# A new preamble for a fused attention and expert kernel: order of loads, rows shared with ScalarE, constant scales, gate bias in bfloat16 parts

## What is computed

```python
def _L0_conv_ref(pair_rep, ln_w, ln_b, wq, wk, wv, wb, wg_w, wg_b, wrep_w, wrep_b):
    x = (pair_rep - mu) * jax.lax.rsqrt(var + EPS) * ln_w + ln_b      # mu, var over all of it
    q, k, v = proj(wq), proj(wk), proj(wv)                            # B, NH=4, C=32, 128, 128
    g = jax.nn.sigmoid(proj(wg_w) + wg_b.reshape(1, NH, C, 1, 1))
    bias = jnp.einsum('hc,bcij->bhij', wb, x)
    scores = jnp.einsum('bhcij,bhcik->bhijk', q, k) * scale + bias[:, :, None, :, :]
    o = g * jnp.einsum('bhijk,bhcik->bhcij', jax.nn.softmax(scores, axis=-1), v)
    return jnp.einsum('oc,bcij->boij', wrep_w, o) + wrep_b.reshape(1, C_Z, 1, 1)

x = x + _L0_conv_ref(_ln_c(x), ...)       # _ln_c: each row of 128, eps 1e-6
t = _to_tokens(x)
t = t + _L0_ffn_ref(_ln_t(t), ...)        # top 2 of 8 experts, 128 -> 512 -> 128, gelu
```

## Time and profile before

| | us |
|---|---|
| median of three runs | 913.08 (911.72 to 914.72) |
| the profiled execution, its own time | 913.78 |
| its span in the trace | 912.0 |
| busy in it: TensorE, VectorE, ScalarE, GpSimd | 621.5, 693.4, 583.5, 416.9 |

### The profile page before, as it was taken

The page is one execution under the profiler, slowest core; times in us unless marked ns, Lnnn a source line. Parts: engine busy times, 40 slices in busy tenths (PEclk is TensorE's granted clock), DMA queues, the critical chain, the costliest instruction groups (busy, mean ns, idle before and its releaser), DMA issues. The chain is left out here.

```text
span 912.0 us, 21482 instructions
## 1 busy us (share of the span) xinstructions
PE 621.5 (68%) x6804; PEld 509.6 (56%) x6804; DVE 693.4 (76%) x2423; ACT 583.5 (64%) x1517; POOL 416.9 (46%) x556
## 2 busy tenths in 40 slices
PE   0006699999998889888888510048999999999100
PEld 0001388877777677776776410047888888888100
DVE  3699579999988998998898369038888888888153
ACT  0015489998998899788878451047788778778100
POOL 3000112221156423545645548717777777777400
PEclk9999689997999899889988555579999999999755
DMA  9933691000000000000000002122322322322499
GB/s 198 222 81 68 193 91 3 3 2 1 2 23 28 26 1 11 26 26 25 31 23 31 28 30 84 45 60 67 84 81 77 83 77 83 81 80 68 92 203 282
DMA packets 61683, 62.01 MB, mean 68 GB/s; under 512 B 20708, under 2 KB 51493, under 8 KB 59912
## 3 DMA queue, kind: packets, MB, share of 16 engines
q1 hardware_dynamic: 51592, 34.28, 18.4%
q0 software_dynamic: 8704, 17.98, 5.9%
q10 hardware_dynamic: 1280, 8.39, 4.2%
HBM read 36.18 MB, written 25.26 MB: 67 GB/s over the span
## 5 line engine op out<-in xcount | busy, mean ns | idle before, releaser
L773 ACT ACTIVATE L<-L,lmin 128x128 f32<-128x128 f32 x512 | 159.6, 398 | 0.2
L700 POOL DMA_INDIRECT expert_out<-yo,rows_all x142 | 140.4, 989 | 41.6 <-issue 21.9
L652 POOL DMA_INDIRECT routed<-pay,pos x128 | 135.6, 1060 | 42.7 <-issue 25.7
L978 DVE CUSTOM_DVE_ANT_0 L<-S,biasN,logit_scale 128x128 f32<-128x128 f32 x512 | 146.1, 346 | 6.3 <-issue 5.8
L631 POOL TENSOR_TENSOR og<-on,rden 128x256 f32<-128x256 f32 x64 | 39.6, 619 | 193.3 <-DVE on L990 191.1
L1225 DVE SCALAR_TENSOR_TENSOR hl<-hf,hscale,hh 128x512 f16<-128x512 f32 x142 | 106.7, 751 | 5.1
L864 ACT ACTIVATE hf<-S,b_sb,inv_hscale 128x256 f32<-128x256 f32 x214 | 105.0, 566 | 2.5 <-PE S L1425 1.5
L620 POOL TENSOR_TENSOR xs<-x,xs 64x512 fp32r<-64x512 f32 x32 | 40.6, 1270 | 126.8 <-ACT xs L749 106.4
L1223 DVE TENSOR_SCALAR hh<-hf,hscale 128x512 f16<-128x512 f32 x142 | 69.6, 490 | 36.7 <-ACT hf L864 29.7
L963 DVE TENSOR_TENSOR pl<-PT,ph 128x512 f16<-128x512 f32 x128 | 84.9, 685 | 13.2 <-ACT ph L768 12.5
L1440 PE MATMUL PT<-w_h,hh 128*128 x568 | 77.8, 218 | 21.5 <-DVE hl L1225 21.5
(11 more groups left out here) (232 smaller groups left out, 1828.1 us busy)
## 6 DMA issues: line engine op xcount, KB each, us to landing
rows_all<-routed SPq DMA_DIRECT2D x71, 132.0 KB
xt<-in_x SPq DMA_DIRECT2D x8, 512.0 KB, 25.6
shared<-in_L_conv_ln_w ACTq DMA_DIRECT2D x8, 512.0 KB, 12.3
shared<-in_L_conv_ln_b ACTq DMA_DIRECT2D x8, 512.0 KB, 10.5
shared<-expert_out SPq DMA_DIRECT2D x16, 256.0 KB, 11.8
pay<-expert_out SPq DMA_DIRECT2D x16, 256.0 KB, 11.3
out<-xt SPq DMA_DIRECT2D x16, 256.0 KB, 9.2
expert_out<-yo,rows_all POOLq DMA_INDIRECT x142
```

The source lines that it names most:

```text
L652: pool.indirect_dma_start(routed, bass.IndirectOffsetOnAxis(ap=pos[:, slot, i:i + 1], axis=0), pay[:, i, :], None).then_inc(scattered[slot ...
L700: pool.indirect_dma_start(expert_out, bass.IndirectOffsetOnAxis(ap=row_place[t % IN_BUFS][:, k, W + 1:W + 2], axis=0), yo[t % YO_BUFS][:, ...
L773: last = nc.scalar.activation(L[p][:, h, i, :], L[p][:, h, i, :], ACT.Exp, scale=-1.0, bias=lmin[p][:, h * R + i:h * R + i + 1])
L978: last = nc.vector.tensor_tensor_reduce(out=L[p][:, h, i, :], in0=S[(4 * u + h) % 3][:, i * P:(i + 1) * P], in1=biasN[:, h, :], scale=logi ...
```

## The change

SP's queue now holds all of x first, then ln_w and ln_b in turn, chunk by chunk, each with a buffer of its own (`lnb_all`) and a semaphore for each chunk; the weights are on ScalarE's queue and the gate bias, three times, on GpSimd's. VectorE takes all statistics first and then one chain of scales over 64 rows. The global scale is multiplied into `rstd2`, and `shift` is minus the mean times it. Of each chunk VectorE does 5 rows and ScalarE 11, then VectorE multiplies by ln_w and adds ln_b. q, k and the gate keep their weights unscaled and split after chunk 1; only v gets a scale, from the sum of squares, which TensorE takes up behind the first scores of unit 0. `logit_scale` and `bias_scale` become constants. The gate bias is held as three bfloat16 parts in rows 0, 32 and 64 of a 65 row operand, and one matmul adds them. ScalarE's list interleaves rows, bias copies and squares, and casts x of unit 0 ahead of the last bias copies.

```diff
+    DVE_ROWS = 5
...
         @block.sync
         def _(sp):
+            def load(into, view, landed, c):
+                for f in range(2):
+                    sp.dma_start(into[f * C:(f + 1) * C, chunk(c), :], view[f, :, chunk(c), :]).then_inc(landed[c], 16)
+
             for c in range(CH):
...
+                load(xt, xv, x_in, c)
+            for c in range(CH):
+                load(shared, lwv, lnw_in, c)
+                load(lnb_all, lbv, lnb_in, c)
...
             chain.link(nc.gpsimd.memset(bg_f, 0.0))
+            for row in range(0, B2_ROWS, 32):
+                pool.dma_start(bg_f[row:row + 1, :], wg_b.rearrange("(o c) -> o c", o=1)).then_inc(bg_in, 16)
...
+            act.wait_ge(rows_known, 1)
+
+            def scale_rows(c):
+                for i in range(c * CR + DVE_ROWS, (c + 1) * CR):
+                    last = nc.scalar.activation(x1[:, i, :], xt[:, i, :], ACT.Identity, scale=rstd2[:, i:i + 1], bias=shift[:, i:i + 1])
+                last.then_inc(rows_scaled, 1)
...
+            for c in range(CH - 1):
+                scale_rows(c)
+            act.wait_ge(w_in, 11 * 16)
...
+            copy_bias(0)
+            scale_rows(CH - 1)
+            copy_bias(1)
+            square_rows(0)
+            copy_bias(2)
+            square_rows(1)
+            high_x(0, 0)
+            copy_bias(3)
...
+                dve.wait_ge(x_in[c], 32)
+                last = row_statistics(c * CR, (c + 1) * CR)
+            chain.link(last)
+            row_scales(chain, slice(0, HALF), 1e-6)
...
+            chain.link(nc.vector.tensor_scalar(rstd2[:], rstd[:], grstd[:, 0:1], None, ALU.mult))
+            nc.vector.scalar_tensor_tensor(shift[:], mean[:], -1.0, rstd2[:], ALU.mult, ALU.mult).then_inc(rows_known, 1)
...
+                for i in range(c * CR, c * CR + DVE_ROWS):
+                    last = nc.vector.tensor_scalar(x1[:, i, :], xt[:, i, :], mean[:, i:i + 1], rstd2[:, i:i + 1],
+                                                   ALU.subtract, ALU.mult)
+                chain.link(last)
+                dve.wait_ge(rows_scaled, c + 1)
+                dve.wait_ge(lnw_in[c], 32)
+                nc.vector.tensor_tensor(x1[:, k, :], x1[:, k, :], shared[:, k, :], ALU.mult).then_inc(lnw_used, 1)
+                dve.wait_ge(lnw_used, c + 1)
+                dve.wait_ge(lnb_in[c], 32)
+                nc.vector.tensor_tensor(x1[:, k, :], x1[:, k, :], lnb_all[:, k, :], ALU.add).then_inc(x1_ready, 1)
...
                 for i in range(R):
                     last = nc.vector.tensor_tensor_reduce(
                         out=L[p][:, h, i, :], in0=S[(4 * u + h) % 3][:, i * P:(i + 1) * P], in1=biasN[:, h, :],
-                        scale=logit_scale[:, 0:1], scalar=BIG, op0=ALU.add, op1=ALU.min,
+                        scale=-float(D) ** -0.5, scalar=BIG, op0=ALU.add, op1=ALU.min,
...
+            def sum_row_squares():
+                pe.wait_ge(sums_ready, 1)
+                nc.tensor.matmul(B[:, 0:2], ones[:], sums[:, 0:2], start=True, stop=True).then_inc(squares_summed, 1)
+                pe.wait_ge(weights_ready, 2)
...
                 if half == 0:
+                    if u == 0:
+                        sum_row_squares()
                     pe.wait_ge(qk_copied, 2 * u + 2)
...
-                for part in (bg_h, bg_l):
-                    last = nc.tensor.matmul(av[:, :, 1, :], ones_r[:], part[:].unsqueeze(1).broadcast_to([P, 2, P]),
-                                            start=False, stop=part is bg_l, **flags)
-                last.then_inc(vg_full, 1)
+                nc.tensor.matmul(av[:, :, 1, :], ones_g[:], bg_parts[:].unsqueeze(1).broadcast_to([B2_ROWS, 2, P]),
+                                 start=False, stop=True, **flags).then_inc(vg_full, 1)
```

More of the change, by code:

```diff
@@ L709, in _ @@
         def _(act):
[L710 to L712 removed]
+            for n, w in enumerate((wq, wk, wv, wg_w)):
                 for f in range(2):
[L714 to L717 removed]
+                    act.dma_start(wraw[:, n, f, :], w).then_inc(w_in, 16)
@@ L726, in _ @@
-            for c in range(2, CH):
-                act.wait_ge(lnw_used, c + 1)
-                for f in range(2):
-                    act.dma_start(lnb_at[c][f * C:(f + 1) * C], lbv[f, :, chunk(c), :]).then_inc(lnb_in[c % 2], 16)
-            for c in range(CH):
+            act.wait_ge(rows_known, 1)
[3 more added lines that the diff above has]
+                last.then_inc(rows_scaled, 1)
@@ L731, in _, with copy_bias, square_rows @@
+            def copy_bias(c):
+                for n in range(c * (CR // R), (c + 1) * (CR // R)):
+                    act.wait_ge(bias_done, n + 1)
+                    nc.scalar.activation(bias_rows[:, n * NQ:(n + 1) * NQ], SG[n % 4][0:2 * NH, :], ACT.Copy).then_inc(bias_copied, 1)
+            def square_rows(c):
                 act.wait_ge(x1_ready, c + 1)
-                for k in range(2 if c < CH // 2 else 0):
+                for k in range(2):
                     last = nc.scalar.activation(square_junk.rearrange("p (r w) -> p r w", w=W),
@@ L915, in _, with split_weights @@
             rsqrt(nc, chain, grstd[:], gstat[:, 1:2], gtmp[:, 0:1], gtmp2[:, 0:1])
-            dve.wait_ge(lnw_used, CH)
+            chain.link(nc.vector.tensor_scalar(rstd2[:], rstd[:], grstd[:, 0:1], None, ALU.mult))
+            nc.vector.scalar_tensor_tensor(shift[:], mean[:], -1.0, rstd2[:], ALU.mult, ALU.mult).then_inc(rows_known, 1)
+            def split_weights(parts):
+                chain.link(nc.vector.tensor_copy(w4h[:, parts, :], w4[:, parts, :]))
+                for f in range(2):
+                    k, other = (slice(g * C, (g + 1) * C) for g in (f, 1 - f))
+                    nc.vector.tensor_scalar(w4l[f][other, parts, :], w4[other, parts, :], 0.0, None, ALU.mult)
+                    last = nc.vector.tensor_tensor(w4l[f][k, parts, :], w4[k, parts, :], w4h[k, parts, :], ALU.subtract)
+                return last
@@ new lines, in _ @@
+                if c == 2:
+                    dve.wait_ge(bg_in, 48)
+                    chain.link(nc.vector.tensor_copy(bg_parts[:], bg_f))
+                    for more in (slice(32, 64), slice(64, 65)):
+                        for _ in range(more.start // 32):
+                            chain.link(nc.vector.tensor_tensor(bg_f[more], bg_f[more], bg_parts[more], ALU.subtract))
+                            chain.link(nc.vector.tensor_copy(bg_parts[more], bg_f[more]))
+                    chain.link(nc.vector.tensor_copy(ones_g[:], ones[0:B2_ROWS, :]))
@@ L936, in _ @@
-            chain.link(nc.vector.reciprocal(inv_scales[:, 0:3], scales[:, 0:3]))
-            chain.link(nc.vector.tensor_scalar(bias_scale[:], scales[:, 0:1], scales[:, 1:2], float(D) ** 0.5, ALU.mult, ALU.mult))
-            chain.link(nc.vector.tensor_scalar(logit_scale[:], inv_scales[:, 0:1], inv_scales[:, 1:2], -float(D) ** -0.5, ALU.mult, ALU.mult))
-            dve.wait_ge(w_transposed, 1)
-            for n in range(3):
-                last = nc.vector.tensor_scalar(w4[:, n, :], PT[0][:, n * P:(n + 1) * P], scales[:, n:n + 1], None, ALU.mult)
@@ L942, in _ @@
-            chain.link(nc.vector.tensor_copy(w4[:, 3, :], PT[0][:, 3 * P:4 * P]))
-            chain.link(nc.vector.tensor_copy(w4h[:], w4[:]))
-            for f in range(2):
-                k, other = (slice(g * C, (g + 1) * C) for g in (f, 1 - f))
-                nc.vector.tensor_scalar(w4l[f][other], w4[other], 0.0, None, ALU.mult)
-                last = nc.vector.tensor_tensor(w4l[f][k], w4[k], w4h[k], ALU.subtract)
-            chain.link(last)
+            chain.link(nc.vector.tensor_copy(gstat[:, 2:4], B[:, 0:2]))
@@ L1241, in _ @@
             pe.wait_ge(const_ready, 1)
-            pe.wait_ge(w_in, 12 * 16)
+            pe.wait_ge(rowvar_ready, 1)
+            nc.tensor.matmul(B[:, 0:1], ones[:], gstat[:, 0:1], start=True, stop=True).then_inc(rowvar_summed, 1)
+            pe.wait_ge(w_in, 11 * 16)
             for n in range(4):
```

111 lines of the change are left out of this document (35 added, 76 removed).

## The result

The changed kernel took 884.79 us (median of 4 runs, 883.92 to 887.6) beside 912.4 for the kernel before: a ratio of 0.971 (95% interval 0.968 to 0.974). In a later group of runs, on another chip, it was 0.9736 (0.9714 to 0.9758). The forecast was 872, its range 860 to 888. So the sign and the size of the preamble were right, and 12.8 us of the whole were not there. The profiled execution took 883.92 us with a span of 882.1.

A forecast was written before the change was run, and what follows sets the result against it. A late-starting VectorE chain bounds the preamble, VectorE the long loop steps, ScalarE the early loop. Span 912.0 less 23.5 (preamble), 1.5 (loop fill), 15 (constant logit scale), 1 (gate bias) is 871.0, so 872 us; range 860 to 888.

The forecast's parts named there:

- the sign: Whole kernel: faster than the kernel before by more than 0.01, chance 0.96; slower 0.03.
- the size of the preamble: Ahead of the attention loop: first logits on VectorE start at 81.1 us instead of 104.63, 23.5 us won.

The follow-up runs named there:

- the shares of rows: Changed kernel with VectorE's rows at 9, 5, 2 and 1 of sixteen in chunks 0 to 3 instead of 5: 880.59 us; with the early scatter too, 836.46 us.
- the last group: Changed kernel (861.05 us) and three variants: x not loaded first (889.46), pointer scale with early scatter (854.51), constant with early scatter and changed rows (836.46); kernel before 884.6.
- the first two groups: Four variants each, of logits' scale, scatter place, gate-bias pass and VectorE's rows, in the kernels before or after; the kernel before took 913.6 and 911.3 us.

## What to carry to other kernels

An engine without a gap in a step is not yet the bound alone: follow back each thing that the next step waits for, here the low cast, and see how far it lies under the busy engine, since that distance bounds what a faster engine wins. Where an engine waits for its own DMA to land, issue that DMA as early as the step allows: here it was worth some 2 us in one kernel, 12 to 15 in the next, and with the shares of rows 25 on the last chip. And when all of a stage hangs on one tensor, load that first: 28 us here.

## What the runs showed that I had not expected

- Packets of instructions take part in the DMA traffic, and GpSimd's wait for a scatter beside a 16 KB one was 1.7 to 3.3 us instead of 1.4.
- The same kernel took 885 us in its first runs and 861 on the chip of the last group. The loop gave 4 of that; the experts 15 (256.8 us from the last scatter of the loop to the last of the experts, and 241.8), with TensorE's waits for `hl` at 18.5 and 4.4 us. What differs there stays open.
- Stalls of up to 2.1 us with no releaser on this core, on ScalarE and VectorE, in the kernel before, in the changed kernel and in all kernels of the first two groups, and in none of the four of the last.
